# Macaron block on one core: POOL takes three of four blocks of the quantized hidden rows, in two operations, and the gate products alternate between two PSUM banks

## The reference

```python
def fp4_quant_dequant(x):            # per block of 16 values
    scale = max(max(abs(xb)) / 6, 1e-12)
    q = GRID[searchsorted(MID, abs(xb / scale))] * sign(xb) * scale
def fp4_linear(x, w): return einsum(fp4_quant_dequant(x), fp4_quant_dequant(w))
gate, y = fp4_linear(x, w_gate), fp4_linear(x, w_up)     # 352 columns
h = silu(gate) * y
x = x + 0.5 * fp4_linear(h, w_down)
```

## Time and profile before

| | us |
|---|---|
| median of 3 runs | 708.93 |
| lowest and highest | 707.54, 710.84 |
| profiled execution, whole | 710.62 |
| its span | 708.5 |
| DVE busy in the span | 586.9 (83%) |
| PE busy, PE weight loads | 646.7 (91%), 464.9 (66%) |
| ACT busy | 451.9 (64%) |
| POOL busy | 315.0 (44%) |

### The profile page before, as it was taken

How to read it: one execution, slowest core, us unless ns; L and a number is a source line. 1 busy time by engine, 2 the same in 40 slices (tenths; PEclk the granted TensorE clock), 3 DMA queues, 4 the chain that set the end, 5 groups by cost and what they waited for, 6 DMA issues and landing times. The chain is left out here.

```text
span 708.5 us, 15987 instructions
## 1 busy us (share of the span) xinstructions
PE 646.7 (91%) x5778; PEld 464.9 (66%) x5778; DVE 586.9 (83%) x1540; ACT 451.9 (64%) x859; POOL 315.0 (44%) x424
## 2 busy tenths in 40 slices
PE   4999999999999989999999698998889987899895
PEld 3777777777878867777776366565565755556564
DVE  2788778966676679987889899999799998999983
ACT  3677779866456517777788466667655535667642
POOL 7100001185655422000012676745978675676520
PEclk9999999999999999999999799999999999999998
DMA  8100000000000000000000000000000000000101
GB/s 211 29 0 0 0 0 1 1 2 4 3 0 2 3 3 0 1 1 1 0 1 1 0 1 1 0 1 1 1 0 2 1 1 1 4 27 16 30 16 30
DMA packets 13464, 7.07 MB, mean 10 GB/s; under 512 B 1304, under 2 KB 13408, under 8 KB 13408
## 3 DMA queue, kind: packets, MB, share of 16 engines
q1 hardware_dynamic: 11328, 5.27, 2.8%
q10 hardware_dynamic: 2080, 1.05, 0.5%
HBM read 4.22 MB, written 2.10 MB: 9 GB/s over the span
## 5 line engine op out<-in xcount | busy, mean ns | idle before, releaser
L1546 PEld LDWEIGHTS ps<-expert_work 128*128 128x128 f32 x1024 | 132.6, 193 | 69.0 <-ACT expert_work L660 47.3
L1161 DVE SCALAR_TENSOR_TENSOR x_sb<-ps,gates,x_sb 128x128 f32 (+1 forms) x512 | 143.4, 342 | 30.2 <-PE ps L1546 22.1
L1546 PE MATMUL ps<-expert_work 128*128 128x128 f32 x1024 | 138.4, 278 | 1.0 <-ACT expert_work L660 1.0
L1546 PE MATMUL ps<-xnT,expert_work 128*128 128x512 f32 x256 | 135.1, 610 | 0.7 <-ACT xnT L641 0.7
L656 ACT ACTIVATE expert_work<-ps 128x512 f32<-128x512 f32 x128 | 75.6, 590 | 52.6 <-PE ps L1546 52.3
L367 POOL TENSOR_SCALAR vareps<-meanvar 128x4 f32<-128x4 f32 (+1 forms) x28 | 9.1, 324 | 222.2 <-DVE meanvar L1075 221.6
L660 ACT ACTIVATE expert_work<-expert_work 128x512 f32<-128x512 f32 x128 | 80.6, 630 | 4.1
L1546 PE MATMUL ps<-gateT,xnT 128*128 128x352 f32 x128 | 57.0, 528 | 14.6 <-ACT ffn_work L791 11.4
L424 POOL TENSOR_TENSOR shared<-shared 128x128 f32<-128x128 f32 x112 | 51.5, 460 | 24.9 <-ACT shared L751 16.7
L1546 PE MATMUL ps<-downT,hqT 128*128 128x128 f32 x384 | 57.2, 287 | 4.2 <-ACT hqT L901 4.0
L634 ACT ACTIVATE xn<-x_sb,shift,rstd 128x128 f32<-128x128 f32 (+1 forms) x132 | 55.4, 481 | 2.7 <-POOL shift L375 2.7
(11 more groups left out here) (180 smaller groups left out, 1330.0 us busy)
## 6 DMA issues: line engine op xcount, KB each, us to landing
x_sb<-in_L_attn_x_dram SPq DMA_DIRECT2D x8, 256.0 KB, 7.3
out_dram<-x_sb SPq DMA_DIRECT2D x8, 256.0 KB, 2.3
expert_work<-in_L_ffn_w_all_dram ACTq DMA_DIRECT2D x2, 512.0 KB, 6.5
wraw<-in_L_attn_qkv_w_dram SPq DMA_DIRECT2D x1, 192.0 KB, 4.5
wraw<-attn_in_proj_weight_dram SPq DMA_DIRECT2D x1, 192.0 KB, 3.4
fraw<-in_L_ffn_w_down_dram SPq DMA_DIRECT2D x1, 176.0 KB, 2.6
fraw<-in_L_ffn_w_gate_dram SPq DMA_DIRECT2D x1, 128.0 KB, 2.1
fraw<-in_L_ffn_w_up_dram SPq DMA_DIRECT2D x1, 128.0 KB, 2.1
```

Of the source, the lines that this page charges most:

```text
L1161: t = nc.vector.scalar_tensor_tensor(tile_b(i, j), bank(4 + e % 4, TPB, C)[:, j, :], gates[:, j, e:e + 1], tile_b(i, j), ALU.mult, ALU.add)
L1546: return nc.tensor.matmul(o, a, b, start=start, stop=stop, **kw)
```

## The change

EARLY goes from 2 to 1. DVE's L1494 then multiplies block 0 alone, and POOL's L479 the blocks 1 to 3 in two operations, block 1 first and then the blocks 2 and 3 together, each with a signal; DVE waits for both, PE for the first before it transposes block 1 and for the second before block 2. In all groups but the first, the gate products use the banks 1, 0, 1, 0 for the blocks 0 to 3, and each waits for the silu that last read its bank. Since bank 0 also takes transposed h, PE waits for the fourth silu of group g+1 before the transposes of block 1 of group g.

```diff
--- before.py
+++ after.py
@@ -37,7 +37,7 @@
 BLK = 16
 NBH = 4 * FI // BLK
 KB = FI // BLK
-EARLY = 2
+EARLY = 1
 LN_EPS = 1e-5
 ATT_EPS = 1e-6
 MAGIC = 1.5 * 2.0 ** 22
@@ -266,9 +266,10 @@
         def tile_fb(g, j):
             return tile_f(False, g, j)
 
-        def late(a):
-
-            return a[:, KB * EARLY:NBH].rearrange("p (j k) -> p j k", k=KB).unsqueeze(3).to_broadcast([P, TPB - EARLY, KB, BLK])
+        def late(a, first, n):
+
+            return (a[:, KB * first:KB * first + KB * n].rearrange("p (j k) -> p j k", k=KB).unsqueeze(3)
+                    .to_broadcast([P, n, KB, BLK]))
 
         def early(a):
             return a[:, 0:KB * EARLY].rearrange("p (j k) -> p j k", k=KB).unsqueeze(3).to_broadcast([P, EARLY, KB, BLK])
@@ -283,6 +284,10 @@
         def v_bank(i):
 
             return 0 if i > 0 else 4
+
+        def gate_bank(j):
+
+            return 1 - j % 2
 
         def known_below(i, n):
 
@@ -476,8 +481,9 @@
                 def h_late(self, g):
 
                     pool.wait_ge(self.s["hq_ready"], g + 1)
-                    nc.gpsimd.tensor_tensor(hq_blocks(EARLY, TPB - EARLY), by_block(fq_h[0], EARLY, TPB - EARLY),
-                                            late(h_max[:, g % 2, :]), ALU.mult).then_inc(self.s["hq_late"], 1)
+                    for first, n in ((EARLY, 1), (EARLY + 1, TPB - EARLY - 1)):
+                        nc.gpsimd.tensor_tensor(hq_blocks(first, n), by_block(fq_h[0], first, n),
+                                                late(h_max[:, g % 2, :], first, n), ALU.mult).then_inc(self.s["hq_late"], 1)
 
                 def x_back(self, g):
 
@@ -784,6 +790,8 @@
                 a.then_inc(s["xn_ready"], 1)
 
             def silu(s, g, j, k=1):
+                if g > 0:
+                    k = gate_bank(j)
                 if j == 0 and g > 0:
 
                     act.wait_ge(s["hid_done"], g)
@@ -1471,7 +1479,7 @@
                     ch.link(nc.vector.tensor_reduce(largest, hid[:, :, :], AX, ALU.max, apply_absolute_value=True))
                     ch.link(nc.vector.reciprocal(h_inv[:, :], largest))
                     if g > 0:
-                        dve.wait_ge(s["hq_late"], g)
+                        dve.wait_ge(s["hq_late"], 2 * g)
                     nc.vector.scalar_tensor_tensor(blocks(v), h3, 6.0 * (1.0 - NUDGE),
                                                    h_inv[:, :].unsqueeze(2).to_broadcast([P, NBH, BLK]),
                                                    ALU.mult, ALU.mult).then_inc(s["h_divided"], 1)
@@ -1568,9 +1576,14 @@
 
                 if j == 0:
                     pe.wait_ge(s["xnT_ready"], g + 1)
-                if g * TPB + j > 0:
-
-                    pe.wait_ge(s["silu_ready"], g * TPB + j)
+                if g > 0:
+
+                    k = gate_bank(j)
+                    if j != 1:
+                        pe.wait_ge(s["silu_ready"], g * TPB + j - (1 if j > 1 else 0))
+                elif j > 0:
+
+                    pe.wait_ge(s["silu_ready"], j)
                 mm(bank(k, FI), tok(j), gateT[:, 0:FI]).then_inc(s["gate_done"], 1)
                 if g > 0 and j == 0:
 
@@ -1983,8 +1996,11 @@
 
             def ffn(s, first, front):
                 def hidden_transposes(g, j):
-                    if j == EARLY:
-                        pe.wait_ge(s["hq_late"], g + 1)
+                    if j in (EARLY, EARLY + 1):
+                        pe.wait_ge(s["hq_late"], 2 * g + 1 + j - EARLY)
+                    if j == 1 and g + 1 < GROUPS:
+
+                        pe.wait_ge(s["silu_ready"], (g + 1) * TPB + TPB)
                     for k in range(3):
                         t = nc.tensor.transpose(bank(6 * (1 - j % 2), 3, P)[:, k, :], hq[:, j, P * k:P * k + P], ident[:, :])
                     t.then_inc(s["htr_done"], 1)
```

## The result

| | before | after |
|---|---|---|
| median of 20 runs each, us | 709.51 | 712.17 |
| lowest and highest | 706.75, 711.74 | 708.12, 715.57 |
| profiled execution, whole | 710.62 | 712.48 |
| its span | 708.5 | 710.7 |

The ratio of after to before is 1.0036, with a 95% interval of 1.0019 to 1.0052. The changed kernel is slower by 2.6 us (1.3 to 3.7 by the interval). The median is 0.7 us from the forecast of 712.9, but a part of that nearness is luck: the forecast added +4.0 to a median of 708.93, the first 3 runs of the kernel before, where all 20 give 709.51. As a difference it is +4.0 forecast against +2.6 measured.

What follows compares the result with a forecast made beforehand. DVE was taken as the bound of the steady feed-forward groups. The terms 4.63 - 0.75 + 0.38 - 0.3 gave +4.0 us on the median 708.93, so 712.9 us, range 705.5 to 716.5.

Steps and rivals of the forecast that it cites:

- Part 1: DVE's multiply L1494 on one block takes 0.37 us less; next L1487 at +12.32 if nothing else is late.
- collision: POOL's L489, due at +8.46, meets DVE's L1475 at +8.37; the two exclude each other; total +4.63 us.
- Part 2: POOL's L479 in two operations: first at +5.01 taking 0.79 us, second at +5.75, so L489 at +8.46.
- B: Step after a case A: POOL's L489 comes first, DVE's L1475 is held to +8.76; step 12.71 us, +0.02.
- case A: DVE's L1475 first, POOL's L489 ends at +10.91, DVE idles 1.28 us at L1487; step 13.60 us, +0.91.
- Part 3: Gates alternating between two banks: 0 in steady steps, -0.75 us in body 6 of the second phase.
- Part 4: Added waits of PE and DVE: cost 0, but +0.38 us in body 6 of the first phase.
- The end: At the very end the first hq_ready comes 0.37 us earlier, of which PE's chain keeps perhaps 0.3: -0.3.
- rival 1: No exclusion at this pair, L489 runs beside L1475: -4.7 us, 704.2 us; chance 0.20.
- rival 2: L489 starts before L1475 and holds DVE: 712.9 us, or 709.5 at the lower bound; chance 0.12.
- rival 3: Case A in every step, if POOL's new operation costs towards 1.39 us: +7.5, 716.4 us; chance 0.13.
- rival 4: Nothing that shows, stalls smaller than worked out: about 708 to 710 us; chance 0.10.

Runs made afterwards that it cites:

- e4: The changed kernel with the reciprocals read by DVE's divide of h placed in PSUM, plus a PE wait; 702.92 us, ratio 0.9906 to before.
- e5: The kernel before with only the reciprocals read by DVE's divide of h moved to PSUM; 710.64 us, ratio 1.0003.
- e6: The changed kernel with ACT's magnitude of h ahead of its copy of x's transposes; 720.02 us, ratio 1.0137 to before.
- e2: The kernel before with only the new split of h (DVE one block, POOL three in two operations), one gate bank; 716.06 us, ratio 1.0095.
- e1: The kernel before with only the two gate banks, DVE and POOL two blocks each; 708.89 us, ratio 0.9976.
- e7: The changed kernel with the new division of h only in groups 6 and 7, two banks everywhere; 707.00 us, ratio 0.9960 to before.
- e8: e4 with two blocks on DVE and two on POOL in group 6 of the first phase; 703.75 us, ratio 0.9909 to before.
- e3: The changed kernel with POOL's three blocks in one operation; 719.95 us, ratio 1.0152 to before.

## Why the prediction was right, point by point

**Part 1 and the bound.** L1502 takes 0.52 (0.51 forecast). With the collision gone a step is 12.33 (e4), so DVE was the bound and the 0.37 was there to be had. Shown.

**Part 2.** POOL's two operations take 2.13 together: the first 0.78 alone (0.79 forecast), the second 1.39, starting 0.74 behind the first. Their start in B is 4.40 behind L1495 (4.39 forecast), that of L492 6.49 (6.48). (The text lets L465 end at +4.98; by the earlier trace rows it is +5.06. Nothing hangs on it, and in case A the first operation starts at +5.01, as forecast.)

**The collision, cases A and B.** From the start of L1495, forecast and measured in A: L1483 8.37 and 8.37; L495's end 10.91 and 10.91; L647 11.69 and 11.72; L579 12.19 and 12.21; the next L1495 13.60 and 13.61. In B: L495's start 7.84 and 7.85; L1483's end 10.38 (8.76 + 1.62) and 10.39; the step 12.71 and 12.72. The text took L1483 as held to 8.76, and the trace shows it starting at 8.38 and taking 2.01; both are the same wait. (In the earlier trace rows L1487 comes 2.25 behind L573, since DVE is busy until then; the 1.41 of the working does not stand there, but after has 1.40, 429.08 to 430.48.) e4 and e5 show that the cause is the exclusion, and that an input's place decides it. By "SBUF — State Buffer", section "Who interferes with whom", in the Trainium skill, a DVE instruction with at most one SBUF input, outside its two-port modes, does not contend with GpSimd; here the trace agrees, with 1.62 and 1.06 side by side (e4) against 1.62 and 2.46 (after). e6 shows the last link, ACT's order, in one step; some 0.25 of the 1.29 is DVE's own wait for the quantized x, which the text had put as hidden.

**The count of A and B.** In bodies 1 to 4 of the first phase the differences are +0.91, +0.01, +0.90, -0.09 where +0.91, +0.02, +0.91, +0.02 stood; body 5 gives -0.21. In the second, bodies 0 to 5 give +0.93, +0.01, +0.92, +0.02, +1.77, -0.82, together +2.83 (2.77 forecast). The 1.77 and -0.82 are one case A and nothing else: before, the L1487 that begins body 5 starts early under a POOL multiply and takes 2.4 instead of 1.6, as the earlier trace rows has it for the first phase; in the second phase of after it does not, which moves 0.8 from one body to the next.

**Body 0** was taken as 0 and is 0.83 shorter (14.29 to 13.46). It runs partly at the low PE clock (granted 0.86 in before), and it scatters between kernels: e5, with the half form and one bank like before, has 13.82, and the kernels with two banks lie between 12.82 and 14.16. The collision is in it as well (L1483 412.06, 2.48 us). How much of the 0.83 is the banks stays open.

**Part 3, mis-sized.** A gate and up pair was priced at 1.41 from a row in which gates still wait for silus. With two banks the products follow each other by 0.59 to 0.60, a pair in 1.2, as PE's timeline after shows:

```profile
429.24 0.86 PE L1554 MATMUL ps<-gateT,xnT 128*128 128x352 f32 x2
429.93 0.76 PE L1554 MATMUL ps<-upT,xnT 128*128 128x352 f32 x2
430.52 0.76 PE L1554 MATMUL ps<-gateT,xnT 128*128 128x352 f32 x2
431.12 0.76 PE L1554 MATMUL ps<-upT,xnT 128*128 128x352 f32 x2
431.71 0.76 PE L1554 MATMUL ps<-gateT,xnT 128*128 128x352 f32 x2
```

(the first pair 0.69 + 0.59, the next 0.60 + 0.59). So the up products end about 0.8 earlier than worked out, and DVE's L1472 in the step behind a case A (434.72 above) has no idle time before it. That case A would cost more without the two banks is borne out by e2. The gain in body 6 of the second phase, forecast as -0.75 out of an idle time of 0.96 and without a sum for it, is -1.42 (12.38 to 10.96): e1 has -1.06 of it from the banks alone, e7 -1.42 with the quarter form too.

**Part 4, mis-sized.** Body 6 of the first phase was to cost +0.38 and cost +1.53 (12.38 to 13.91). POOL is as late there as worked out (its last multiply ends 7.70 behind L1495 instead of 7.33), but it was priced as a delay of the chain at the same speed. The timeline and the stretch behind it, after:

```profile
487.50 2.13 POOL L485 TENSOR_TENSOR hq<-ffn_work,h_max 128x352 f32<-128x352 f32 x2
488.34 0.55 PE L2005 MATMUL ps<-ident,hq 128*128 128x128 f32 x3 [2.00 <-POOL hq L485]
...
491.64 0.85 PE L2005 MATMUL ps<-ident,hq 128*128 128x128 f32 x3
```

```profile
488.30:492.90 4.60, 4.44 (x24) 4.25 (x25) 4.53 (x11) 2.78 (x7) 1.33 (x1) 0.66 0.00 0
```

PE stood 2.00 us, and its granted clock over the next 4.6 us is 0.66, a part of them at the lower level: the same three transposes take 0.85 instead of 0.49. In e8, where PE waits 1.09, the 4.6 us behind it have a granted clock of 1.00 and the body takes 12.29. e4 has the quarter form and nearly the same wait as after, but no fall of the clock:

```profile
484.49 0.55 PE L2007 MATMUL ps<-ident,hq 128*128 128x128 f32 x3 [1.87 <-POOL hq L485]
```

```profile
484.45:489.05 4.60, 4.29 (x33) 3.75 (x33) 4.53 (x11) 3.98 (x11) 1.33 (x1) 1.00 0.00 0
```

Its body 6 takes 12.66, which is +0.28 against before where +0.38 was forecast. So the forecast priced the wait about rightly, and the other 1.25 us of after go with the low clock. Why the clock fell after one wait and not after the other stays open.

**The end** was to give -0.3 and gave -0.92. From body 7 to the end of the span the kernels with the quarter form there, in two operations, have 13.45 to 14.45 (six of them, mean 13.92), those with the half form 14.45 to 14.83 (before, e1 and e5, mean 14.70), and e3, in which block 1 is late, 15.53. So the term is nearer to -0.8, with a scatter as large; its mechanism was not followed further.

**The sum.** Two phases and the end were forecast at +4.0 and are +2.7 in the profiled pair. The misses are body 0 (-0.83), body 6 of the second phase and the end (-0.67 and -0.62), body 6 of the first (+1.15) and -0.28 in the other bodies, together -1.25: they partly cancel, so the total is nearer than its parts, and that is luck. What is not luck is the chain of the collision, which was forecast to a few hundredths and makes +4.35 of the account against 4.63. The rivals: rival 1 is refuted by after. e4 shows what it would have been worth: the bodies with steady steps and their neighbours give -4.19 where the rival has -4.1, and the total is -6.7 where it has -4.7, as body 0 (-0.97) and body 6 of the second phase (-1.38) give more; rival 2, L489 first, is what e2 and e3 settle into; rival 3 did not come; rival 4 is not it, since each stall of the working is in the trace.

**Expectations that failed.** e3 and e6, both for one reason: an instruction was moved or merged for the wait that ends last, and the engine that stands on its other end (PE, for block 1; PE again, for the transposed x) was not asked.

## What to carry to other kernels

When work is moved off the bounding engine, look at which instructions of DVE and POOL it slides over each other. Here, where both read SBUF and the DVE one had two such inputs, the overlap was a lock (1.62 and 2.46 us instead of 1.62 and 1.06), and its price ran through whoever waited for the loser; with the smaller input in PSUM both ran side by side, and that turned a loss of 0.4% into a gain of 0.9%. Before merging or reordering, follow both ends of the instruction: in a fixed order, an engine's early small piece can be what keeps a third engine's queue moving. And a new wait of PE in a busy stretch is to be priced with the granted clock that may follow it, not by its length alone.

## What was not expected of the hardware

- A few hundredths separate the two orders: DVE is first by 0.08 in case A of after, POOL by 0.05 in e3. Each start recurs step after step, as one step sets the next.
- The one that came second is not fully idle meanwhile: L495 ends 0.92 after L1483 (427.78 and 426.86) though it takes 1.06 alone, and L1483 in e3 ends at 440.87, 1.48 after L495's end at 439.39, though it takes 1.62 alone. So 0.14 of it does not come on top, in both orders.
- A matmul of 128x352 that needs no freed bank follows the one before by 0.59 to 0.60 us; the first of a chain by 0.69.
- Waits of PE: 2.00 us (after and e7) was followed by 4.6 us at a granted clock of 0.66 and 0.63; 1.87 us in e4, at the same place, by a stretch at 1.00. Length alone does not decide it: 1.95 us in e6 was followed by 3.4 us at 0.52 after a first 1.4 us at 0.97, but 2.12 us in a steady step of e3 by 4.6 us at 1.00. What tells them apart was not tried.
